# Single-head cross attention in a two-layer Perceiver kernel: Wq·Wkᵀ folded inside the first normalisation's block, the context loaded two tiles ahead, column-tiled matmuls in round order

## What is computed

```python
# stage A: layer norm (no gain, no shift), then cross attention with one head; x += out
def _layernorm(x, axis=-1, eps=1e-05):
    m = jnp.mean(x, axis=axis, keepdims=True)
    v = jnp.var(x, axis=axis, keepdims=True)
    return (x - m) / jnp.sqrt(v + eps)

def _L0_xattn_ref(q_in, k_v, Wq, bq, Wk, bk, Wv, bv):
    q = q_in @ Wq + bq
    k = k_v @ Wk + bk
    v = k_v @ Wv + bv
    sim = jnp.einsum('bid,bjd->bij', q, k) * SCALE
    attn = jax.nn.softmax(sim, axis=-1)
    out = jnp.einsum('bij,bjd->bid', attn, v)
    return out
# stages B to F: self attention, experts, cross attention with 16 heads,
# low-rank self attention, experts
```

## Time and profile before

| what | us |
|---|---|
| median of three runs (lowest, highest) | 2437.06 (2435.38, 2444.72) |
| the profiled execution, its own time | 2455.45 |
| its span in the trace | 2453.7 |
| stage A in the trace, to the first instruction of stage B on DVE | 205.9 |
| of it: start and normalisation, to the first projection matmul | 28.0 |
| of it: projections, to the first instruction of the attention block | 85.7 |
| of it: attention over eight tiles, to the first instruction of stage B | 120.2 |

### The profile page before, as it was taken

How to read it: one execution, slowest core, us unless ns; L and a number is a source line. 1 busy time by engine, 2 the same in 40 slices (tenths; PEclk the granted TensorE clock), 3 DMA queues, 4 the chain that set the end, 5 groups by cost and what they waited for, 6 DMA issues and landing times. The chain is left out here.

```text
span 2453.7 us, 39271 instructions
## 1 busy us (share of the span) xinstructions
PE 2102.0 (86%) x14020; PEld 1784.9 (73%) x14020; DVE 1126.3 (46%) x2057; ACT 898.0 (37%) x1479; POOL 926.3 (38%) x638
## 2 busy tenths in 40 slices
PE   6895888837999973999999999977665999999994
PEld 5543777637999962688888888865544999999993
DVE  4245463765555537222223322348754445544543
ACT  2112121214666642233333333223222555555551
POOL 2002312105777763222222222213212666666654
PEclk9996999957999986999999999968876999999997
DMA  3482000016888874011100100010003566656653
GB/s 124 178 312 108 18 19 33 1 35 238 277 278 279 280 230 175 23 33 27 35 26 26 31 31 26 18 48 5 22 22 129 198 217 213 211 198 217 214 194 124
DMA packets 102452, 299.03 MB, mean 122 GB/s; under 512 B 10912, under 2 KB 27936, under 8 KB 102336
## 3 DMA queue, kind: packets, MB, share of 16 engines
q1 hardware_dynamic: 76928, 232.88, 28.3%
q0 software_dynamic: 11840, 38.81, 5.1%
q10 hardware_dynamic: 13600, 26.22, 2.9%
HBM read 265.10 MB, written 32.77 MB: 121 GB/s over the span
## 5 line engine op out<-in xcount | busy, mean ns | idle before, releaser
L134 PE MATMUL banks<-ra 128*128 128x256 f32 (+3 forms) x3004 | 983.6, 328 | 65.9 <-DVE x L1040 24.3
L135 PE MATMUL banks<-ra 128*128 128x256 f32 (+3 forms) x3004 | 968.9, 323 | 0.1
L136 PE MATMUL banks<-ra 128*128 128x256 f32 (+3 forms) x3004 | 965.1, 321 | 3.4 <-issue 3.1
L134 PEld LDWEIGHTS banks<-ra 128*128 128x128 f32 (+1 forms) x3004 | 578.9, 193 | 131.8 <-issue 50.4
L136 PEld LDWEIGHTS banks<-ra 128*128 128x128 f32 (+1 forms) x3004 | 578.7, 193 | 45.2 <-issue 1.3
L135 PEld LDWEIGHTS banks<-ra 128*128 128x128 f32 (+1 forms) x3004 | 580.0, 193 | 39.0 <-issue 3.1
L1475 POOL TENSOR_TENSOR ra<-fa,ra 128x1024 fp32r<-128x1024 f32 x187 | 446.3, 2387 | 237.3 <-ACT ra L1508 236.3
L1508 ACT ACTIVATE ra<-fa 128x1536 fp32r<-128x1536 f32 x190 | 281.5, 1482 | 85.4 <-DMA fa<-in_L_units 68.2
L1592 DVE TENSOR_TENSOR ra<-fa,ra 128x256 fp32r<-128x256 f32 x190 | 162.1, 853 | 92.0 <-ACT ra L1532 91.5
L332 POOL TENSOR_TENSOR ra<-fa,ra 128x2048 fp32r<-128x2048 f32 (+2 forms) x22 | 85.7, 3905 | 285.3 <-ACT ra L326 278.6
L1567 DVE TENSOR_TENSOR ra<-fa,ra 128x512 fp32r<-128x512 f32 x190 | 133.6, 703 | 115.8 <-ACT ra L1508 109.0
(11 more groups left out here) (219 smaller groups left out, 2505.3 us busy)
## 6 DMA issues: line engine op xcount, KB each, us to landing
fa<-in_L_units SPq DMA_DIRECT2D x190, 768.0 KB, 4.5
fa<-in_ctxT SPq DMA_DIRECT2D x64, 514.0 KB, 4.1
ea_y_scratch<-fa ACTq DMA_DIRECT2D x35, 512.0 KB
fa<-in_ctx SPq DMA_DIRECT2D x32, 512.0 KB, 5.3
eb_y_scratch<-fa ACTq DMA_DIRECT2D x15, 512.0 KB, 3.6
fa<-in_L_attn_w_qkvT SPq DMA_DIRECT2D x6, 1024.0 KB, 7.3
normed_scratch<-na SPq DMA_DIRECT2D x16, 256.0 KB, 2.1
x<-in_x SPq DMA_DIRECT2D x1, 2048.0 KB, 8.6
```

The source lines that it names most:

```text
L134: pe.matmul(psum, lh, rh, start=first, stop=False)
L135: pe.matmul(psum, lh, rl, start=False, stop=False)
L136: return pe.matmul(psum, ll, rh, start=False, stop=last)
```

## The change

The function `cross_one_head` is rewritten, and the block at the start is taken into it.

- **One block in the place of three.** Start, normalisation and projections are one block now. SP issues, without waits between them, Wqᵀ, Wkᵀ, x, Wv, the first tile's transposed context, and, when the two weights' low parts are made, the first tile's context rows. The biases are issued by ACT.
- **The fold.** PE makes M = Wq·Wkᵀ from the weights alone (48 matmuls) and a row u = bk·Wqᵀ (12), before it transposes the first tiles. Then qp = xn·M + Wk·bq, 8 jobs of 12 matmuls in the place of 16. Wk·bq takes 32 narrow matmuls, one set in the place of two. `shift` becomes (x − mean)·u·rstd + bq·bk on DVE, two instructions of 512 a tile. The low parts of Wq and Wk are made by DVE, that of Wv by POOL near the end of the block.
- **Two tiles ahead.** `ct`, `cn` and `cl` have two buffers each. The loads for tile n+2 wait once for all scores, or all of p_ctx, of tile n.
- **Round order.** In scores and in p_ctx the chunk is the outer loop and the sequence the inner one, behind one group of waits.
- The area `ra` of the later stages is allocated after stage A. 14 more semaphores are cleared behind stage B.

```diff
+                    @block.sync
+                    def _(eng):
+                        eng.dma_start(staging[0], columns(d["L0_xattn_WqT"])).then_inc(s_wq, 16)
+                        eng.dma_start(staging[1], columns(d["L0_xattn_WkT"])).then_inc(s_wk, 16)
+                        eng.dma_start(x[:], d["x"].rearrange("(t p) d -> p t d", p=P)).then_inc(s_x, 16)
+                        eng.dma_start(staging[2], columns(d["L0_xattn_Wv"])).then_inc(s_wv, 16)
+                        load_turned(eng, 0, 0)
+                        eng.wait_ge(s_ql, 1)
+                        eng.wait_ge(s_kl, 1)
+                        load_rows(eng, 0, 0)
...
+                    @block.scalar
...
+                        eng.wait_ge(s_ur, 1)
+                        act.activation(u_row, banks[:, 0, :], ACT.Copy).then_inc(s_urk, 1)
+                        for c in range(DC):
+                            if c == 2:
+                                eng.wait_ge(s_mom, NT)
+                                act.activation(root, moments[:, :, 1], ACT.Sqrt, bias=epst[:]).then_inc(s_root, 1)
+                            eng.wait_ge(s_fold, c + 1)
+                            act.activation(m[0][:, c, :], banks[:, MB + c, :], ACT.Copy).then_inc(s_mh, 1)
...
+                    @block.vector
...
+                        for n in range(NT):
+                            eng.wait_ge(s_hi, n + 1)
+                            own = slice(n * P, (n + 1) * P)
+                            dve.tensor_tensor(xl[:, :, own], chunks(banks[:, n % L, :]), xh[:, :, own].bitcast(F32),
+                                              ALU.subtract).then_inc(s_lo, 1)
+                            if n + L < NT:
+                                normalise(n + L)
...
+                        for j, (h, c) in enumerate(jobs):
+                            eng.wait_ge(s_mm, j + 1)
+                            dve.tensor_scalar(qp[:, c, h * HALF:(h + 1) * HALF], banks[:, MB + j % 4, :], through_k[:, c:c + 1],
+                                              None, ALU.add).then_inc(s_out, 1)
...
+                            links.link(dve.scalar_tensor_tensor(away, x[:, j, :], moments[:, j, 0:1], u_row, ALU.subtract,
+                                                                ALU.mult))
+                            links.link(dve.reduce_sum(shift[:, j:j + 1], away, AX_X))
...
+                        with eng.Fori(0, NT // 2 - 1) as i:
+                            for u in range(2):
+                                n = 2 * i + u
+
+                                eng.wait_ge(s_sc, SEQ * n + 3 * SEQ)
+                                load_turned(eng, n + 2, u)
+
+                                eng.wait_ge(s_pv, SEQ * n + 2 * SEQ)
+                                load_rows(eng, n + 2, u)
...
+                            for j in range(SEQ):
+                                eng.wait_ge(s_ctxT[u][j], 16 * k + 16)
                             for c in range(DC):
-                                ins = pe.matmul(banks[NQ * j:NQ * j + NQ, u, 0:S], qg[u][:, c, NQ * j:NQ * j + NQ],
-                                                ct[j][:, c, :], start=c == 0, stop=c == DC - 1)
-                            ins.then_inc(s_sc, 1)
...
+                                for j in range(SEQ):
+                                    ins = pe.matmul(banks[NQ * j:NQ * j + NQ, u, 0:S], qg[u][:, c, NQ * j:NQ * j + NQ],
+                                                    ct[u][j][:, c, :], start=c == 0, stop=c == DC - 1)
+                                    if c == DC - 1:
+                                        ins.then_inc(s_sc, 1)
```

More of the change, by code:

```diff
@@ L348, in cross_one_head @@
+            cl = [f.take(D) for _ in range(2)]
             f3 = f.at
[L349 to L352, removed]
-            q = [r.take(DC, HALF) for _ in range(2)]
-            load, high, low, s_w = split_programs("xa", [
-                (*wq, columns(d["L0_xattn_Wq"])), (*wk, columns(d["L0_xattn_WkT"])),
-                (*wv, columns(d["L0_xattn_Wv"]))], staging)
@@ L357, in cross_one_head @@
-            s_ctxT = [sem(f"xa_ctxT{j}") for j in range(SEQ)]
-            s_sc, s_bk = sem("xa_scores"), sem("xa_bk_split")
-            def load_turned(eng, n):
-                for j in range(SEQ):
-                    if not (isinstance(n, int) and n == 0):
-                        eng.wait_ge(s_sc, SEQ * n + (SEQ + 1 + j))
-                    eng.dma_start(ct[j], d["ctxT"][SEQ * n + j]).then_inc(s_ctxT[j], 16)
-            layer_norm("na", ahead=((load, high, low), (0, 1, 2), (0,)))
-            s_b, s_mm, s_hi, s_out = sem("xa_biases"), sem("xa_product"), sem("xa_high"), sem("xa_taken")
@@ L456, in cross_one_head @@
-            f = Area(fa, F_SIZE, f2)
-            cn = [f.take(2, D) for _ in range(SEQ)]
-            cl = f.take(D)
+            cn = [[Area(fa, F_SIZE, f2 + 2 * D * j).take(2, D) for j in range(SEQ)], None]
+            u_row, away = f.take(D), f.take(D)
+            n_area = Area(na, N_SIZE)
+            xn = [n_area.take(D) for _ in range(4)]
+            root = n_area.take(NT)
+            s_ctxT = [[sem(f"xa_ctxT{u}{j}") for j in range(SEQ)] for u in range(2)]
+            s_ctx = [[sem(f"xa_ctx{u}{j}") for j in range(SEQ)] for u in range(2)]
@@ L459, in cross_one_head @@
+            made.add("statistics")
+            r = Area(ra1, R_CROSS, r_values)
+            at = [(r.take(DC, P), r.take(DC, P)) for _ in range(2)]
             f = Area(fa, F_SIZE, f3)
-            r = Area(ra, R_SIZE, r2)
-            qg = [f.take(DC, P) for _ in range(2)]
+            qg = [Area(fa, F_SIZE, f2 + 2 * DC * D + DC * P * u).take(DC, P) for u in range(2)]
             pr = [f.take(S) for _ in range(2)]
```

584 lines of the change are left out of this document (318 added, 266 removed).

## The result

The changed kernel takes 2418.1 us (median of 4 runs, 2414.7 to 2420.9), the kernel before on the same chip 2438.0 (4 runs). The ratio is 0.990, with the interval 0.9875 to 0.993. The forecast was 2395, range 2384 to 2410: the direction was right, but only half of the 42 us came, and the result lies outside the range.

What follows compares the result with a forecast made beforehand. PE bounds the attention turn (12.19 us), transfers close behind (11.1). First block 60.0 plus attention 103.2 ends stage A at 163.2, 42.7 earlier; clears cost 0.9, so −41.8 from 2437.06 gives 2395.3, range 2384 to 2410.

Steps and rivals of the forecast that it cites:

- PE's first matmul: First block: Wq lands at 5.8, ACT's high part 1.9, biases' parts 1, DVE's low part 2.5, so PE starts at 11.2.
- 96 projections: First block: 96 projection matmuls on PE at 0.2265 us each, 21.7 us.
- DVE's tail and the lock: End of first block: about 3 us of DVE work behind the last job, plus 0.8 from POOL's lock on DVE.
- block start to scores(7): Attention block: transfers up to tile 7's ctxT, 27.4 MB, 72.0 us at 380 GB/s plus 2.2 for issue and landing: 74.2.
- scores(7) to the end of values(5): End of attention block: one PE turn of 9.6 us after ctxT(7) lands.
- last p_ctx: End of attention block: p_ctx(7) takes 3.0 us (1.05 + 1.94), where before it took 6.0, waiting for its rows.
- Does the queue ever run empty? … So no.: Attention loads: rows of tile n+2 wait some 5 us after ctxT(n+1) lands, with 11 us of transfers still queued.
- rival 2: Attention transfers are slower, 352 GB/s: ctxT(7) lands at 80.0, 5.8 us more, total 2401; chance 0.11.
- Rival 3: Attention turns: the clock falls to 0.50 in half of every turn, turn 13.1, 13.6 us more, total 2409; chance 0.09.
- I give them 1 us, with 0 and 4 as ends: First block: delay from the biases' small parts, which stand ahead of Wq's low part on DVE and wait for three loads.
- rival 4: Scores and p_ctx: groups run one by one, turn 27.4, total 2520, chance 0.02; milder, scores take 3.9, turn 11.5.
- The offset to the median: Whole kernel: median 18.4 us below the profiled execution, so the same −41.8 is taken from the median 2437.06.

Runs made afterwards that it cites:

- the clock held up: The changed kernel's stage A alone with 40 unread matmuls, 16 behind the last projection, 24 behind the first tile's scores: 183.3 us against 184.5.
- fewer bytes: The changed kernel's stage A alone, loading only two of ctxT's four chunks from the third tile on: 176.1 us against 183.6 on another chip.
- the other order: The changed kernel's stage A alone, with tile 0's probabilities and p_ctx(0) ahead of scores(1): 179.0 us against 183.6 on another chip.

## Why the prediction was wrong

**The gain of stage A, 29.0 in the place of 42.7.** The working's own steps, with what the trace has in their place (forecast → after):

| step | error, us |
|---|---|
| PE's first matmul 11.2 → 13.54 | +2.3 |
| from there to the turned tiles 23.3 → 24.4 (u row 4.4 → 5.3) | +1.1 |
| 96 projections 21.7 → 23.5: clock 0.90 from 38 to 48, then 0.233 each, not 0.2265 | +1.8 |
| DVE's tail and the lock 3.8 → 3.0 | −0.8 |
| block start to scores(7) 74.2 → 79.9 | +5.7 |
| scores(7) to the end of values(5) 9.6 → 11.6 | +2.0 |
| the add ahead of the last probabilities 3.2 → 3.2 | 0 |
| last p_ctx 3.0 → 5.4 | +2.4 |
| from there to stage B 13.2 → 12.4 | −0.8 |
| sum | +13.7 |

**The step that failed is "Does the queue ever run empty? … So no."** I reckoned p_ctx(n) some 5 us behind ctxT(n+1) against 11 us of transfers still queued. Both numbers were wrong in the same direction. In the steady loop the rows' load comes 6.9 us behind the scores at the high clock (122.13 to 129.06) and 9.9 at the low one (98.48 to 108.42); and 4.2 MB at the real 0.405 MB a us are 10.4 us. For the first tile there is next to no margin: p_ctx(0) stands behind scores(0), the wait for tile 1 and scores(1). Its rows' load is issued 20.1 us behind the block's start (at 84.59), and what is ahead of it in the queue has moved after 17; even with the clock held up it was 16.1, and 1.5 more pass until its first bytes move. I had worked out the steady turn and taken it for the first. Two experiments show the cause from two sides: the other order takes the first stop away and 4.7 us with it; the clock held up brings p_ctx(0) 4.2 us forward and takes away most of that stop.

**The rate was under-, not overestimated.** Full engines moved 398 GB/s over 30 us (112 to 142) and 409 over 18 (88 to 106) against my 380; 27.4 MB at 0.405 and 2.2 are 69.9 us. ctxT(7) landed after 79.2 (its last load is issued at 133.3 and takes 10.4), so the stops cost about 9 us, and the better rate hid 4. The 0.7 from there to scores(7), at 79.9, are PE's: these scores show no wait for a transfer and stand behind a p_ctx(5) at the low clock (2.77 in the place of 1.93). The Trainium skill's figure behind rival 2 ("DMA: Bandwidth & Descriptors", "Where 436 GB/s comes from", about 358 GB/s from HBM a core) did not bind in this trace, with one core at work, as the 398 over 30 us show. The earlier trace rows already had 405 over 10 us, and I had let 371, the loop's mean at full share, pull my value down.

**Rival 3, the clock, was real but priced as part of a turn.** I let it decide only if a turn passed 11.1 and argued that a late PE works without gaps. It struck where PE waits longest: ahead of the first scores (3.83), of scores(1) (3.22) and scores(3) (4.41), and at the end (2.36, then p_ctx(7) 3.64 in the place of 1.94); and twice in a turn without such a wait (p_ctx(5) took 2.77, p_ctx(6) 3.28). "Which in the trace brought 1.00 back within 4 us" had a row against it: from 104 to 110 PE was busy without a gap, 6.00 of 6.00 us, at 0.50. Its price is not the slow matmuls but the load behind them. It was no price of the round order: the groups' overlap is there at both clocks, 3.66 us at 0.50 and 1.95 at 1.00.

**The first block.** "I give them 1 us, with 0 and 4 as ends" was the right doubt with the wrong value: 2.9. The block's 4.45 lie just outside the range of −2.5 to +4 that I gave. DVE's 2.28 for the low part (2.5 forecast), the fold's 0.227 a matmul and the 32 narrow matmuls (3.6 against 3.65) held. So did the lock: DVE's L478 took 2.50 in the place of 0.74 while POOL's L395 was at work, and PE lost nothing by it.

**What held:** round order at 2.0 (1.95), rival 4 excluded, transfers as the bound of the later turns, PE's own turn (10.2 with fewer bytes), the clears as next to nothing (29.0 at the end of stage A, 28.9 behind them). Against rival 4's milder form, the Trainium skill's rule on weight loads of the same row group ("TensorE: Matmul & The Clock Gate", "The mechanism"), the 32 instructions took 1.95, not 3.9.

**The offset to the median.** This is the second step that failed. "No row says where, so I take the same difference from it": I carried the 18.4 us between the profiled execution of before and its median over to the changed kernel; there it is −3.4. Of the 22.8 us between 2395.3 and 2418.1, 13.7 are stage A's and the other 9 lie in this term. Most of the 18.4 was one event. Near the end of stage C the profile of before holds a standstill of DVE and ACT of 20 us; the profile of the changed kernel has none, a second profile of it has one of 18.6:

```profile
917.50 0.39 ACT L1528 ACTIVATE fa<-banks 128x256 f32<-128x256 f32 x1 [19.83 <-remote]
```

```profile
887.47 0.39 ACT L1614 ACTIVATE fa<-banks 128x256 f32<-128x256 f32 x1 [18.61 <-DMA fa_cross<-in_ctx]
```

The first is of the kernel before, the second of the changed kernel's other profile. The releasers named at its end (a remote one, a load of stage A) can't be its cause. PE does not stand still, it trickles: 19 matmuls from 900 to 917, with gaps in which it waits for nothing that the profile shows, while POOL runs one indirect DMA behind the other:

```profile
906.21 0.37 PE L134 MATMUL banks<-ra 128*128 128x256 f32 x1 [1.82 <-issue]
```

Its cause is open. What it costs can be read, by setting the same instruction of the two traces side by side from stage B on. The changed kernel leads by 29.0 at the start of stage B, by 29.0 just ahead of the standstill, by 46.9 at its end and by 40.3 at the first instruction of stage D:

```profile
896.37 0.39 ACT L1528 ACTIVATE fa<-banks 128x256 f32<-128x256 f32 x1 [1.89 <-remote]
...
957.11 1.28 ACT L273 ACT_TABLE_LOAD   x1 [31.08 <-PEq L106]
```

and in the changed kernel:

```profile
867.36 0.38 ACT L1614 ACTIVATE fa<-banks 128x256 f32<-128x256 f32 x1
...
916.80 1.28 ACT L252 ACT_TABLE_LOAD   x1 [37.02 <-PEq L107]
```

So the standstill costs 11 us of the span, not 20: the end of stage C catches up part of it. The 40.8 us between the two spans are 29.0 of stage A and these 11, and nothing came back in later stages. That the profiled execution took 2414.7, one us from my 2413.7, is luck: stage A gained 13.7 less than I said, and a standstill of which I knew nothing fell away.

**What stays open.** The whole kernel gains 20 to 25 us by the medians, stage A 29 to 32 in the whole kernel's traces and 33 to 35 alone. The intervals (17 to 30, and 18 to 31) touch these numbers but lie low. The moved area is excluded, and so is a loss in later stages as far as traces tell: the kernel before with only the area moved, whose profile has no standstill (span 2444.9), is 33.9 behind the changed kernel at the start of stage B and 31.7 at the end, on another chip. That profile is 3.7 above its median and the changed kernel's 3.4 below its own, so the spread of single executions may be all of the difference; how often the standstill strikes each kernel was not measured.

## What to carry to other kernels

Before writing "the queue never runs empty", follow the loads of the first two turns one by one: the buffers' release in the prologue is later than in the loop, and what is queued must outlast the wait for the next buffer at the low clock, not the high one. Add the time from a load's issue to its first bytes, about 1.5 us here. Where a load waits for an instruction of an engine whose clock is low behind its own waits, the two feed each other; release buffers with the earliest work that can be put first. And a difference between a profile and its median is a finding to look for in the trace, not a constant to carry over.

## What was unexpected of the hardware

- Column-tiled matmuls in round order overlap four abreast at both clocks: 32 of 257 columns in 1.95 us at 1.00 and 3.66 at 0.50; with the eight instructions of a sequence in a row the same 32 take 4.62.
- One core's loads ran at 398 GB/s over 30 us, and at 409 over 18, while PE was at work.
- The load of `bv` (256 KB) let DVE start at 8.2 in stage A alone (first matmul at 12.0) and at 9.5 to 9.8 in the whole kernel (13.5 and 13.2) and with stages A to C (13.3), from the same instructions.
- A standstill of 20 us on DVE and ACT cost 11 us of the span.
- Waits of 3.2 to 4.4 us were each followed by matmuls at the granted clock of 0.50, those of 0.69 and 1.23 ahead of scores were not. Below that the trace gives no rule: p_ctx(6) ran at 0.50 behind waits of 1.21.
